# A DLRM tower: the lookups' transposes cut into row halves, each half with a PSUM bank of its own

## The reference

```python
e = stack([tbl_f[ids[:, f]] for f in range(32)], axis=1)      # 512 x 32 x 64
h = e
for i, (W, b) in enumerate(layers):                           # O = 128 in each
    nxt = einsum('bjk,bzk,ojz->bok', h, e, W.reshape(O, Hj, 32)) + b[None, :, None]
    h, o = (nxt[:, :64], nxt[:, 64:]) if i < 2 else (None, nxt)
    outs.append(o)
z = concatenate(outs, axis=1).sum(axis=2)                     # 512 x 256
x = concatenate([z, dense_ctx], axis=1)
y = relu(relu(x @ W_top1 + b_top1) @ W_top2 + b_top2) @ W_top3
```

## Time and profile before

| | |
|---|---|
| median of 3 runs | 657.89 us (657.76 to 658.94) |
| the profiled execution | 655.34 us |
| its span in the trace | 653.6 us |
| mean granted clock of TensorE over the span | 0.987 |
| TensorE busy | 624.6 us |
| VectorE busy | 483.5 us |
| ScalarE busy | 214.2 us |

### The profile page before, as it was taken

One profiled execution on the slowest core, in us unless ns is written; L12 is line 12 of the kernel. 1 busy time (PEld: TensorE's weight loads), 2 busy tenths in 40 slices (PEclk: granted clock), 3 DMA queues, 4 the chain that ended last, 5 costly groups with the idle time before them and its releaser, 6 DMA issues.

```text
span 653.6 us, 32258 instructions
## 1 busy us (share of the span) xinstructions
PE 624.6 (96%) x14488; PEld 516.1 (79%) x14488; DVE 483.5 (74%) x497; ACT 214.2 (33%) x354; POOL 127.9 (20%) x137
## 2 busy tenths in 40 slices
PE   6657999999999999999999999999999999999998
PEld 6645788888888888878888888888888888888773
DVE  4548888888888888878888888888888888841000
ACT  2314333344433433433233333332333333332012
POOL 7764434354445444000000000000000000000000
PEclk9769999999999999999999999999999999999999
DMA  5111111111111111000000000000000000011000
GB/s 183 28 23 31 25 24 26 23 31 28 26 28 29 27 21 28 13 15 13 11 12 11 11 12 11 12 12 12 12 12 12 12 12 12 12 39 45 11 1 0
DMA packets 31659, 14.87 MB, mean 23 GB/s; under 512 B 24178, under 2 KB 28898, under 8 KB 31379
## 3 DMA queue, kind: packets, MB, share of 16 engines
q1 hardware_dynamic: 27442, 10.26, 7.3%
q0 software_dynamic: 4192, 4.25, 2.9%
HBM read 8.03 MB, written 0.00 MB: 12 GB/s over the span
## 4 chain that ended last, share of the span: by engine, by line
PE 91%; POOL 4%; issue 2%; DVE 1%; ACT 1%; DMA 1%; POOLq 0%; DVEq 0%; ACTq 0%
PE psT L440 20%; PE psX L383 20%; PE psT L464 8%; PE psT L424 8%; PE psT L450 7%; PE psT L427 6%; PE psX L424 4%; PE psX L427 4%; POOL G_sb L249 4%; PE psX L394 3%; PE psX L511 2%; PE psX L403 1%; PE psX L283 1%; PE psT L525 1%; PE psX L541 1%
## 5 line engine op out<-in xcount | busy, mean ns | idle before, releaser
L440 PE MATMUL psT<-T_sb,W1d 64*64 64x256 f32 x1024 | 234.3, 379 | 0.0
L444 PE MATMUL psT<-T_sb,W1d 64*64 64x256 f32 x1024 | 234.3, 379 | 0.0
L450 PE MATMUL psT<-T_sb,W1d 64*64 64x256 f32 (+3 forms) x2048 | 205.4, 300 | 0.0
L730 DVE TENSOR_TENSOR prod<-X 128x1024 f32 (+3 forms) x208 | 171.3, 891 | 15.2 <-PE psT L427 14.9
L767 DVE STREAM_TRANSPOSE PT<-prod 128x4608 f32<-128x4608 f32 x31 | 154.0, 4968 | 0.0
L440 PEld LDWEIGHTS psT<-T_sb,W1d 64*64 64x64 f32 x1024 | 131.3, 133 | 27.8 <-issue 14.4
L464 PE MATMUL psT<-T_sb,W1d 64*64 64x64 f32 (+2 forms) x1536 | 141.7, 270 | 0.0
L444 PEld LDWEIGHTS psT<-T_sb,W1d 64*64 64x64 f32 x1024 | 131.4, 133 | 0.0
L383 PE MATMUL psX<-PT,W0T 32*64 32x256 f32 x4464 | 128.5, 377 | 2.6 <-issue 2.4
L383 PEld LDWEIGHTS psX<-PT,W0T 32*64 32x64 f32 x4464 | 113.7, 131 | 20.5 <-issue 18.9
L450 PEld LDWEIGHTS psT<-T_sb,W1d 64*64 64x64 f32 x2048 | 123.6, 133 | 0.8
(11 more groups left out here) (86 smaller groups left out, 551.5 us busy)
## 6 DMA issues: line engine op xcount, KB each, us to landing
X<-T_sb SPq DMA_DIRECT2D x64, 64.0 KB, 2.0
kept<-grams SPq DMA_DIRECT2D x128, 16.5 KB
G_sb<-in_L_rec_W SPq DMA_DIRECT2D x2, 1024.0 KB, 6.6
E_q<-in_tbl,ids_g POOLq DMA_INDIRECT x96
prod<-in_W_top SPq DMA_DIRECT2D x2, 512.0 KB, 3.6
G_sb<-in_L_rec_W SPq DMA_DIRECT2D x1, 512.0 KB, 5.7
G_sb<-in_tbl,ids POOLq DMA_INDIRECT x32, 2.4
dT<-dT SPq DMA_DIRECT2D x3, 32.0 KB
```

Source lines behind the costliest of these rows:

```text
L440: mm(psT[low, 0, 0:HF * SMP], W1d[low, HF + k, :], cross.rearrange("p v (z y) s -> p v z y s", y=HF)[:, :, :, k, :], start=start, stop=sto ...
L444: mm(psT[high, 0, 0:HF * SMP], W1d[low, k, :], T_flat[low, SMP * row:SMP * (row + HF)], start=start, stop=stop, tile_position=(0, C))
L450: last = mm(out[:, SMP * 4 * a:], W1d[high, HF * v + k, :], T_flat[high, SMP * (row + 4 * a):SMP * (row + HF)], start=start, stop=stop and ...
L730: return tt(out, x[:, :, z0:z0 + nz].unsqueeze(3).broadcast_to(shape), x[:, :, y0:y0 + ny].unsqueeze(2).broadcast_to(shape), ALU.mult)
```

## The change

The X transposes of the 12 lookup steps become eight pieces: for each pair of fields one of the lower 64 partitions of `E_q` (tile position (0, 0)) and one of the upper 64 (tile position (64, 0)), with 64 columns of the identity. The lower rows' results go to bank 2 of psX, the upper rows' to bank 3, each in the first half of the bank. An increment of `turns` stands behind the wait for the rows. `x_copy` reads the two halves of the samples from the two banks in place of two column ranges of one. The prologue's transposes stay whole; their banks are only viewed in another order of dimensions.

```diff
--- before.py
+++ after.py
@@ -168,13 +168,16 @@
 
         block = ctx.enter_context(nc.Block())
 
-        FIRST_X = [psX[:, 2, :], psX[:, 3, :], psX[:, 0, :], psT[:, IN_BANK.index("x3") % 4, :]]
+
+        FIRST_X = [bank.rearrange("p (a h s) -> p h a s", h=2, s=C)
+                   for bank in (psX[:, 2, :], psX[:, 3, :], psX[:, 0, :], psT[:, IN_BANK.index("x3") % 4, :])]
+        LATER_X = psX[:, 2:4, 0:FQ // 2 * C].rearrange("p h (a s) -> p h a s", s=C)
 
         def x_copy(copy, odd, bank, first_tile, first_field):
-            rows = bank[C * odd:C * odd + C].rearrange("p (a h s) -> p h s a", h=2, s=C)
+            rows = bank[C * odd:C * odd + C]
             to = X_fields[:, bass.ds(first_tile, C), bass.ds(first_field + odd, FQ // 2, step=2)]
             for h in range(2):
-                last = copy(to[C * h:C * h + C], rows[:, h])
+                last = copy(to[C * h:C * h + C], rows[:, h].rearrange("p a s -> p s a"))
             last.then_inc(x_evac[odd], 1)
 
         T_BANKS = [psT[:, 2:4], psX[:, 0:2], psT[:, 0:2], psX[:, 2:4], psT[:, 2:4], psX[:, 0:2], psT[:, 0:2], psT[:, 2:4]]
@@ -280,9 +283,17 @@
 
             def x_transposes(rows, bank):
                 for a in range(FQ // 2):
-                    last = nc.tensor.transpose(bank[:, P * a:P * a + P],
-                                               rows[:, 2 * a:2 * a + 2, :].rearrange("s f k -> s (f k)"),
+                    last = nc.tensor.transpose(bank[:, :, a, :], rows[:, 2 * a:2 * a + 2, :].rearrange("s f k -> s (f k)"),
                                                ident[:, :])
+                last.then_inc(x_tr, 1)
+
+            def later_x_transposes():
+                for a in range(FQ // 2):
+                    for h in range(2):
+                        r = slice(C * h, C * h + C)
+                        last = nc.tensor.transpose(LATER_X[:, h, a, :],
+                                                   E_q[r, 2 * a:2 * a + 2, :].rearrange("s f k -> s (f k)"),
+                                                   ident[r, r], tile_position=(C * h, 0))
                 last.then_inc(x_tr, 1)
 
             def weight_bank(what, k, bank):
@@ -482,7 +493,8 @@
                 h_transposes(n + 1)
                 if lookups:
                     pe.wait_ge(rows_in, 16 * FQ * (n + 1))
-                    x_transposes(E_q, psX[:, 3, :])
+                    pe.sem_inc(turns, 1)
+                    later_x_transposes()
                 g2_matmuls(n, 4, HF)
                 if lookups:
                     for evac in x_evac:
@@ -630,7 +642,7 @@
                     first_field = act.snap((n % QUARTERS) * FQ)
                     act.wait_ge(x_tr, QUARTERS + n + 1)
                     for odd in range(2):
-                        x_copy(copy, odd, psX[:, 3, :], first_tile, first_field)
+                        x_copy(copy, odd, LATER_X, first_tile, first_field)
                 g2_copy(n)
                 g0_copy(n + 1)
                 t_copies(n + 1)
```

## The result

The changed kernel took **651.42 us**, the median of 4 executions (649.95 to 653.23), against 657.83 us of the kernel before beside it (4 executions): ratio **0.9914**, 95% interval 0.9894 to 0.9934. The profiled execution took 649.95 us, its span 648.2.

A forecast was written before the change was run, and what follows sets the result against it. TensorE was taken to bound the kernel, with the X transposes fully on its path. Only the pieces gain, 12 x 0.34 = 4.1 us; other terms nothing: median 657.89 to 653.8 us, range 652.8 to 655.7.

The forecast's parts named there:

- What bounds the kernel: TensorE in lookup steps: X transposes cost the path their full 0.59 us a step, 7.1 us over twelve steps.
- The eight pieces: Last H transpose to G2: four pairs at 0.063 us, stretch from 0.74 to 0.40, giving back 0.34 a step.
- The increment: Behind the wait for rows on TensorE: costs nothing; upper bound 0.14 us a step.
- the wait: Gathered rows ahead of the X transposes: met in time, with 1.9 us to spare in the tightest step.
- the second bank: Bank 2 of psX, now written too: no new wait, nothing.
- the copies: X copies on ScalarE: 1.56 us of work under 3.3 us of cover, so they stay hidden; nothing.
- The sum: All twelve lookup steps: 12 x 0.34 = 4.1 us less.
- the first: Rival at the X pieces: TensorE runs dry at the increment, 0.14 us more a step, 655.5 us; chance 11%.
- the second: Rival at the X pieces: row halves do not run together, 3.5 us slower, 661.4 us; chance 4%.
- the third: Rival at Gram and t stages: waits on VectorE lose all 4.1 us, giving 657.9; chance 5%.
- the 107 of the estimate: TensorE weight load: the Trainium skill's time by columns, 107 ns whatever the rows.
- I leave that offset: Whole-run time: the median's 2.55 us above the profiled execution is kept, so 651.2 becomes a median of 653.8.

The follow-up runs named there:

- run with one row half: Changed kernel without the four pieces of the upper rows, so half of the samples' X is left as it was: 653.05 us, ratio 0.9937.
- the run with the pieces apart: Changed kernel with the eight pieces and their wait moved four rounds of G2 later, away from the H transposes: 655.95 us, ratio 0.9983.
- the run with nine increments: Kernel before with nine increments at the start of TensorE's program, no transposes changed: 657.84 us, ratio 0.9998.

## Why the prediction was right and where it was wrong

**What bounds the kernel** was right: the X transposes lay on the path with their whole length, and what they lost the step lost. The stretch fell by 0.33 and the step by 0.35, which agree within what the place of the code moves.

**The eight pieces** were right in size, 0.06 a pair and 0.41 for the stretch against 0.40 forecast, and right in the reason: the same form, so no standing time. The run with one row half shows that halves overlap fully. The forecast had the shared form and the overlap in one sum and didn't say which was the larger; the rows do. Ahead of the first operation the time falls from 0.15 to 0.06, from the first start to the last from 0.39 (0.66 - 0.27) to 0.20, and from the last to G2 from 0.20 to 0.15. Of the 0.33, the shared form is worth 0.13 to 0.14 by the run with the pieces apart; the other 0.19 or so comes from smaller pieces, of two halves at once, in place of whole transposes.

**The increment, the wait, the second bank, the copies** were rightly taken as nothing: the increment alone left 0.74, no row shows TensorE waiting at the pieces, and the copies kept their 1.56 us. No run had the second bank without the rest of the change.

**The sum**, 4.1 us, was 4.17 in the two traces. **The rivals** fell: the first by the 0.06 ahead of the pieces, the second by the pairs 0.06 apart and by the one-half run, the third by the lookup steps of 17.06. What spoke for the second is so, but does not decide: a load is not shorter for having half the rows (139 ns with 64, 141 with 128; both more than the 107 of the estimate), yet eight loads and their pieces fit into 0.20 us, so the loads of the two halves share their time.

**What failed** is the last step, from the profiled execution to the median and its range: "I leave that offset" and "the three runs shown lie within 1.2 us of each other, so the range goes 1 us below the forecast". It took the scatter between executions for some 1 us and gave no reason for the 2.55 us between the profiled execution and the median, which had already said otherwise. The 82 executions of the kernel before lie from 654.58 to 661.19, the 19 of the changed one from 649.95 to 656.8. A part of this scatter is the granted clock, which the forecast called no term in the lookup steps. In steps 2 to 12 it was none; ahead of them and in the first it differs from execution to execution (0.92 against 1.00 in the rows above), and with the mean granted clock the times differ by some 4 to 6 us. The first measurement was low by luck: three of its four executions were at the highest clock, and the two later medians don't repeat it. A median of four can well be 1.5 us off: it was 651.42 at first, then 653.07 and 653.39, and the 19 executions together give 653.07, against the forecast's 653.8. The range should have been at least as wide as that offset, 2.55 us to each side; it would just have taken in 651.42.

Of the 0.5 us by which 4.65 exceeds 4.1, about 0.25 goes with the place of the code (shown by one profile of the run with nine increments). The rest is less than these runs can tell from nothing: at equal clock the difference lies between 4.2 and 5.1 us where more than one execution of the changed kernel counts.

## What to carry to other kernels

Place a small TensorE operation beside one that uses the array in the same form, and cut it to that form: here the shared form was worth some 0.13 of the 0.33 us by which the stretch fell, and the same pieces, put where they cut another stage in two, gained next to nothing. Where an operation used only half of the rows, the other half was free at the same time. And before a range is written around a median, look at how far the profiled execution lies from it: that distance is a sample of the scatter. The mean granted clock of each execution then tells whether two medians were taken under like conditions.

## What the runs showed that was not expected

Pieces of the two row halves overlap even where four of one half stand in the program ahead of four of the other: 0.46 us to G2, against 0.41 with halves in turn. The scatter between executions lies in the prologue and in the first lookup step, which has one or two waits of 0.9 to 1.9 us and in two profiles a granted clock of 0.92, while the eleven steps that follow, together 187.6 us, agree to 0.05 us between three profiles of the changed kernel. And nine instructions far ahead of the loops shortened the first step of the second loop by 0.4 us.
